# Attention rows of a four-layer GNN gathered in earlier stages; ScalarE copies the turned weights, Pool the node strips, key rows in bf16

## The reference

```
two_edge = concatenate(split(edge_attr, 2, axis=-1), axis=0)   # 50000 x 128
out_idx = concatenate([receivers, senders], axis=0)            # with 25000 edges of the record
logits = sum(two_edge * node_attr[out_idx], axis=1) / sqrt(128)
seg_max = segment_max(logits, out_idx)
ex = exp(logits - seg_max[out_idx])
denom = segment_sum(ex, out_idx)
agg = segment_sum(two_edge * ex / denom[out_idx], out_idx)
x = concatenate([agg, node_attr], axis=1) @ W + b
```

## Time and profile before

| | us |
|---|---|
| median of 3 runs | 6680.08 (6674.97 to 6690.29) |
| the profiled execution | 6675.12 |
| its span in the trace | 6673.5 |
| pair counts, 1453 to 1973 | 520 |
| source pass, each of three | 256 |
| GCN normalisation | 86 |
| attention side D, side S | 545, 544 |

### The profile page before, as it was taken

The page is one execution under the profiler, slowest core; times in us unless marked ns, Lnnn a source line. Parts: engine busy times, 40 slices in busy tenths (PEclk is TensorE's granted clock), DMA queues, the critical chain, the costliest instruction groups (busy, mean ns, idle before and its releaser), DMA issues. The chain is left out here.

```text
span 6673.5 us, 88566 instructions
## 1 busy us (share of the span) xinstructions
PE 3400.8 (51%) x20818; PEld 2597.0 (39%) x20821; DVE 3893.5 (58%) x13711; ACT 1143.2 (17%) x3927; POOL 3040.9 (46%) x3168
## 2 busy tenths in 40 slices
PE   1000200036644765466468889789567666632333
PEld 0000000024433554355345545455566656632333
DVE  9100910079985877577765473464677767774444
ACT  0000000015541111011100000000155545520000
POOL 2776277702323775477400000000077767724775
PEclk9999999978875555555578889789788878865555
DMA  6000000014443443344354464454043344311112
GB/s 281 3 3 20 6 3 3 3 46 132 133 117 80 106 105 61 85 102 102 53 114 89 86 130 84 82 114 89 12 108 105 98 98 104 105 30 40 50 49 45
DMA packets 802920, 512.99 MB, mean 77 GB/s; under 512 B 591282, under 2 KB 707036, under 8 KB 798684
## 3 DMA queue, kind: packets, MB, share of 16 engines
q1 hardware_dynamic: 702044, 351.52, 20.8%
q0 software_dynamic: 100608, 158.42, 11.2%
HBM read 384.62 MB, written 125.12 MB: 76 GB/s over the span
## 5 line engine op out<-in xcount | busy, mean ns | idle before, releaser
L738 POOL DMA_INDIRECT attD_g<-in_edge_attr,attD_ring x416 | 395.3, 950 | 1681.5 <-ACT attD_ring L752 1559.6
L738 POOL DMA_INDIRECT fild_g<-table,fild_ring x416 | 426.9, 1026 | 298.2 <-ACT fild_ring L752 173.0
L196 POOL DMA_INDIRECT recordsS<-sortS_rS,sortS_addrS x416 | 425.4, 1023 | 262.8 <-DVE sortS_addrS L237 136.4
L738 POOL DMA_INDIRECT gatBp_g<-table_head,gatBp_ring x416 | 415.2, 998 | 242.2 <-issue 124.6
L738 POOL DMA_INDIRECT gatAp_g<-table_heads,gatAp_ring x416 | 408.5, 982 | 251.4 <-ACT gatAp_ring L752 126.2
L196 POOL DMA_INDIRECT recordsD<-sortD_rD,sortD_addrD x392 | 401.2, 1023 | 221.8 <-issue 119.1
L738 POOL DMA_INDIRECT attS_g<-in_edge_attr,attS_ring x416 | 396.2, 952 | 149.7 <-issue 122.2
L802 PE MATMUL fild_ps<-fild_g,fild_oh 128*128 128x128 f32 x832 | 213.3, 438 | 394.3 <-DMA fild_g<-table,fild_ring 288.5
L698 PE MATMUL pairs_p_b<-pairs_blk,pairs_oh 128*128 128x256 f16 x1024 | 280.8, 304 | 184.5 <-DVE pairs_oh L685 165.1
L661 POOL DMA_DIRECT2D pairs<-pairs_blk x256 | 159.1, 622 | 431.4 <-ACT pairs_blk L713 422.0
L802 PEld LDWEIGHTS fild_ps<-fild_g,fild_oh 128*128 128x128 f32 x832 | 185.3, 328 | 422.2 <-DVE fild_oh L854 176.4
(11 more groups left out here) (655 smaller groups left out, 10291.6 us busy)
## 6 DMA issues: line engine op xcount, KB each, us to landing
gcnw_strip<-pairs SPq DMA_DIRECT2D x150, 800.0 KB, 5.9
pairs<-pairs_blk SPq DMA_DIRECT2D x768, 64.0 KB, 1.5
pairs<-sortD_blank SPq DMA_DIRECT2D x27, 1600.0 KB, 37.9
gatAp_rowb<-locD SPq DMA_DIRECT2D x104, 256.0 KB, 3.3
gatBp_rowb<-locD SPq DMA_DIRECT2D x104, 256.0 KB, 3.2
attD_rowb<-locD SPq DMA_DIRECT2D x104, 256.0 KB
attS_rowb<-locS SPq DMA_DIRECT2D x104, 256.0 KB, 3.4
pairs<-pairs_blk POOLq DMA_DIRECT2D x256, 64.0 KB, 1.9
```

The lines of the kernel that those rows point to most:

```text
L196: pool.indirect_dma_start(self.rec_dram, bass.IndirectOffsetOnAxis(ap=self.addr[:, c:c + 1], axis=0), self.r[:, c, :], None, bounds_check= ...
L738: pool.indirect_dma_start(rows(u, k), None, table, bass.IndirectOffsetOnAxis(ap=ring[:, u, k:k + 1], axis=0)).then_inc(gathered[u], 16)
```

## The change

All 832 attention gathers leave the attention passes. They are done in earlier stages, in groups of four as before (208 groups: 104 of side D, then 104 of side S), into a small ring `held_attr` in SBUF, and from there SP stores each group (256 KB) to a DRAM table `attrD` or `attrS`, in the order in which it is wanted. 56 groups go to the pair counts, 46 to each source pass, 14 to the GCN normalisation. The attention pass loads them back by plain DMAs of SP.

```
+FETCH = {"pairs": 56, "source": 46, "norm": 14}
+HOLD = {"pairs": 8, "source": 6, "norm": 6}
+    def gather(self, pool, k):
+        n = self.first + k
+        side, slot, turn = "DS"[n // NG], k % HOLD[self.kind], k // HOLD[self.kind]
+        if turn:
+            pool.wait_ge(self.put[slot], 16 * turn)
+        for q in range(G):
+            ...
+            pool.indirect_dma_start(self.held[:, slot, q, :], None, self.table,
+                                    bass.IndirectOffsetOnAxis(ap=rows, axis=0)).then_inc(self.landed[slot], 16)
+
+    def store(self, eng, k):
+        slot, turn = k % HOLD[self.kind], k // HOLD[self.kind]
+        eng.wait_ge(self.landed[slot], 16 * G * (turn + 1))
+        eng.dma_start(attr_group(self.C, self.first + k), self.held[:, slot]).then_inc(self.put[slot], 16)
+
+    def all_stored(self, eng):
+        for slot in range(HOLD[self.kind]):
+            eng.wait_ge(self.put[slot], 16 * len(range(slot, FETCH[self.kind], HOLD[self.kind])))
```

**Pair counts.** The loops of SP and Pool are written out. Pool, after its store of item g (and before it waits for item g + 1):

```
+                while done < (g + 1) * FETCH["pairs"] // NG_ITEMS:
+                    attr.gather(pool, done)
+                    done += 1
```

**Source passes and normalisation.** Pool runs `attr.gather(pool, k)` for k in 0 to 45 (0 to 13), and nothing else. SP stores between its strip loads:

```
             for i in range(LOADS, NT):
                 sp.wait_ge(summed, i - LOADS + 1)
                 sp.dma_start(held(i), by_source[i]).then_inc(strip_in[i % LOADS], 16)
+                while done < (i - LOADS) * FETCH["source"] // (NT - LOADS):
+                    attr.store(sp, done)
+                    done += 1
+            for k in range(done, FETCH["source"]):
+                attr.store(sp, k)
+            attr.all_stored(sp)
```

**Attention pass.** SP loads keys and rows into a slot; the keys are now bf16 (128 KB instead of 256 KB), as is `pen`:

```
+                    sp.wait_ge(pen_ready, nth(i - 1, u))
+                    sp.wait_ge(acc_done, nth(i - 1, u))
+                    load(i, u)
```

The node strips (`hts`) go from ACT to Pool, which waits for the products of two groups before. The copy of the turned weights (`wt`) goes from DVE to ACT, and the index copies (L752) are gone from here:

```
-            def take_weights(i, u):
-
-                dve.wait_ge(weights_turned, nth(i, u))
-                nc.vector.tensor_copy(wt[:, u % 2], p_w[:]).then_inc(wt_ready, 1)
...
+            def take_weights(i, u, before=U):
+                if before >= 2:
+                    act.wait_ge(acc_done, nth(*behind(i, u, -2)))
+                act.wait_ge(weights_turned, nth(i, u))
+                nc.scalar.copy(wt[:, u % 2], p_w[:]).then_inc(wt_ready, 1)
```

More of the change, by code:

```diff
@@ L648, in count_pairs @@
         block = ph.block()
[L650 to L664, removed]
+        attr = AttrFetch(nc, C, ph, a, "pairs", FIRST["pairs"])
         @block.sync
@@ L1066, in _, with attention_pass @@
             turns(pe, step)
-def attention_pass(nc, C, name, side, table, ht, acc, run, cont):
+def attention_pass(nc, C, name, side, ht, acc, run, cont):
     W = F + 1
@@ L1104, in _, with take_nodes, load @@
         def _(pool):
-            gather_groups(nc, pool, ring, indexed, table, lambda u, k: g[:, u, k, 0:F], gathered, acc_done)
+            def take_nodes(i, u, before=U, left=U):
+                nt = node_tiles(pool, C, side, i, u)
+                if before >= 2:
+                    pool.wait_ge(products, nth(*behind(i, u, -2)))
+                for k in range(G):
+                    last = nc.gpsimd.tensor_copy(hts[:, u % 2, k, :], ht[:, bass.ds(nt[k], 1), :].squeeze(1))
+                last.then_inc(hts_ready, 1)
+            turns(pool, take_nodes)
         @block.sync
         def _(sp):
-            load_key_rows(sp, C.loc[side], rowb, rows_loaded, pen_ready)
+            keys = C.loc[side]
+            def load(i, u):
+                loc = keys[tiles(i, u), :].rearrange("t p -> (t p)").partition_broadcast(P)
+                sp.dma_start(rowb[:, u, :], loc).then_inc(rows_loaded[u], 16)
+                rows = C.attr[side].rearrange("(n p g) f -> n p g f", p=P, g=G)[bass.ds(i * U + u, 1)].squeeze(0)
+                sp.dma_start(g[:, u, :, 0:F], rows).then_inc(gathered[u], 16)
+            for u in range(U):
+                load(0, u)
+            with sp.Fori(1, NG // U) as i:
+                for u in range(U):
+                    sp.wait_ge(pen_ready, nth(i - 1, u))
+                    sp.wait_ge(acc_done, nth(i - 1, u))
+                    load(i, u)
         @block.vector
@@ L1199, in take_rows, with step @@
                 nc.scalar.copy(gt[:, u % 2], p_g[u % 2][:]).then_inc(gt_ready, 1)
[L1201 to L1205, removed]
-            def step(i, u, before=U, left=U, index_next=True):
+            def take_weights(i, u, before=U):
+                if before >= 2:
+                    act.wait_ge(acc_done, nth(*behind(i, u, -2)))
+                act.wait_ge(weights_turned, nth(i, u))
+                nc.scalar.copy(wt[:, u % 2], p_w[:]).then_inc(wt_ready, 1)
+            def step(i, u, before=U, left=U):
                 if left >= 1:
-                    take_nodes(*behind(i, u, 1))
                     take_rows(*behind(i, u, 1))
@@ L1252, in multiply, with sums @@
                 last.then_inc(products, 1)
-            def sums(i, u):
+            def sums(i, u, before=U):
+                if before >= 2:
+                    pe.wait_ge(acc_set, nth(*behind(i, u, -2), G) + 1)
                 pe.wait_ge(wt_ready, nth(i, u))
@@ L1265, in step @@
                 if before >= 2:
-                    sums(*behind(i, u, -2))
+                    sums(*behind(i, u, -2), before=before - 2)
                 if before >= 1:
@@ L1731, in held, with _ @@
             return strip[:, (NT + i) % LOADS]
+        @block.gpsimd
+        def _(pool):
+            for k in range(FETCH["source"]):
+                attr.gather(pool, k)
         @block.sync
         def _(sp):
+            done = 0
             for i in range(LOADS, NT):
@@ L1911, in gcn_layers, with _ @@
             block = ph.block()
+            attr = AttrFetch(nc, C, ph, a, "norm", FIRST["norm"])
+            @block.gpsimd
+            def _(pool):
+                for k in range(FETCH["norm"]):
+                    attr.gather(pool, k)
+            @block.sync
+            def _(sp):
+                for k in range(FETCH["norm"]):
+                    attr.store(sp, k)
+                attr.all_stored(sp)
             @block.scalar
@@ L1984, in attention_layer @@
         for side in "DS":
[L1985 removed]
+            attention_pass(nc, C, name + side, side, ht, accs[side], run[side], cont[side])
         with Phase(nc, name + "a") as ph:
```

97 lines of the change are left out of this document (63 added, 34 removed).

## The result

The changed kernel takes 6447.7 us (median of 4 runs, 6446.6 to 6449.0), the kernel before 6679.2 us in the same comparison: ratio 0.9651, 95% interval 0.9634 to 0.9668. 231 us are gone, where 155 were forecast.

The account below looks back on a forecast made before the run. Pool's gathers were taken to bound both attention passes, DVE the pair counts. Attention -300, source passes +72, normalisation +28 and pair counts +45 gave -155 from 6675, or 6520, set at 6525 us for the median; range 6410 to 6790.

Parts of the forecast that it names:

- Attention, -150 each: Both attention passes: without Pool's gathers, 104 steps of 3.6 us plus 20 make 395 us instead of 545.
- The chain: Attention step: multiply, greatest, running maximum, then the next multiply; without the weight copy 3.3 us from group to group.
- a clock of 0.86: Attention passes: PE's average granted clock, making its 3.4 us of work 3.9; the step was taken as 3.6.
- The step of the weight copy: Attention step: the 0.68 us copy on DVE delays the first greatest; without it, that starts 0.1 us after the multiply.
- Pool's copies: Attention step: four copies on Pool at 0.293 us plus gaps, 1.2 to 2.4 us, under the 3.6 us step.
- The waits that were added: Attention passes: `acc_set` and `acc_done` look two groups back, cost nothing; up to 0.35 us per step if DVE fell behind.
- Source passes, +24 each: Three source passes: Pool does 6 groups, stops for the full ring, then does 40; 280 us instead of 256.
- Normalisation, +28: GCN normalisation: 16 DVE products each hold back a gather; 19 to 22 of 56 left over; ends +10 and +35.
- the tail, put at 4 us: End of the normalisation: a landing and a store, 4 us, behind 24 us of gathers left over.
- Pair counts, +45: Pair counts: DVE, the bound, delayed at most 0.23 us by each of 224 gathers, 52 us; ends 0 and +60.
- SP's loop: Pair counts: SP ended its stores 12.5 us after Pool's last; it gets 56 more issues but loses its loop.
- The starved gathers: Rival, pair counts: DVE's one-hots starve gathers, as one 21.0 us store suggests; +300 instead of +45, 6780 us; chance 0.27.

Follow-up runs that it names:

- the version without gathers: The kernel before, with only SP's and Pool's programs in the pair counts written out instead of looped, without a gather there: 6666.9 us, ratio 0.9988.

## Why the prediction was right, and where its terms were off

The forecast was 6525, in a range of 6410 to 6790, faster at 0.65; it came out 6448. The mechanism was right: the attention passes were bound by Pool's gathers, these fitted elsewhere, and what was lost elsewhere was a part of it. Part of the closeness is luck: the attention passes gave 49 us more than forecast and the pair counts took 41 less, while GAT and the normalisation took 19 more. By its steps:

- **Attention, -150 each; measured -174 and -175.** The chain was put at 3.3 us and steps of the changed kernel are 3.41 on average. The step that failed is the one after it, where 3.3 was raised to 3.6 for a clock of 0.86; that is 20 of the 24 us. That clock was one of the kernel before; it was 0.98 once PE no longer stood waiting for rows. It was read as a property of the work and is one of the waiting. That 3.41 lies near 3.3 does not show the chain at work: PE, busy 3.15 us per step, waits for its end in 13 steps of 104.
- **The step of the weight copy** was right in kind (it had to leave DVE) and wrong in reason. In the chain, as the prediction had it (the first greatest 0.35 us later), it would have cost 36 us per pass; in side D it cost 7. It was worth 97 us in side S, most likely for the fetches of code. The prediction had no such term, and as the change made the copy leave, this did not show in the result; with both copies at their old owners the kernel is at 6550.
- **Pool's copies** cost nothing, as said. The waits that were added were put at nothing too. They are met: `acc_set` holds PE's weight loads in 86 of 104 steps, 39.7 us in side D. Whether that lengthens the step was not tested.
- **Source passes, +24 each; measured +24, +24, +23.** Six groups, a stop of 36.2 us, then 40 groups: as worked out.
- **Normalisation, +28; measured +36**, just over the end of +35. 16 products held back 16 gathers, and 36 of the 56 were done when DVE ended, where 37 were forecast. The mis-sized term is the tail, put at 4 us: from the last gather's end at 4865.1 to the next stage at 4876 there are 11 us, for its landing (up to 9.9 us in this stage) and its store.
- **Pair counts, +45; measured +4.** The term was 0.2 us of DVE delay for each gather. DVE's busy time grew by 2.7 us in all. What the gathers do cost, 15 us, comes behind DVE: Pool's last store ends 7 us later than in the version without gathers, four gathers stand behind it for 5, and SP's stores run on to 1974.1, 6 us after them; from there to the next stage it is 3 us less. And 11 us came back: 8 from SP's loop, which the prediction named and did not count, and 3 as no store was held.
- **The starved gathers**, the rival on the slower side with 0.27, did not come: 977 ns in the median, 1061 at most. Its main row was one store out of 256. What it read in that row was right, as two more stores of the same kind show, each held until DVE stopped; what was wrong is to expect it of every gather. Beside one-hots of some 0.27 us nearly every gather and store gets in; beside products of 3.49 us none did.
- **GAT pass A, +17**, had no term in the sum. The keys in bf16 did it: 571 us with them, 555 and 552 without in two runs. In the changed kernel Pool's 416 gathers are busy 427.6 us there and 408.5 before. Two kernels with the same GAT code were at 566. The trace shows what they meet. 86 of the gathers take over 1.1 us, and each of them ends 0.7 to 0.9 us after one of DVE's two operations of 0.68 us with both inputs in SBUF: 42 after the product `gatAp_msg`, 44 after the comparison `gatAp_oh`. Before there were 52 such gathers, 11 of them after `gatAp_msg`. The shorter penalty moves DVE's work in time, and more gathers start beside that product; that this is the way from the one to the other is argued, not tested. One case:

```profile
2106.45 0.68 DVE L1030 TENSOR_TENSOR gatAp_msg<-gatAp_g,gatAp_msg 128x512 f32<-128x512 f32 x1
...
2106.69 1.26 POOL L796 DMA_INDIRECT gatAp_g<-table_heads,gatAp_ring  x1 [0.30 <-issue]
```

## What to carry to other kernels

A granted clock that is read from a stage bound by waiting is not the clock of that stage once the wait is gone; price the new step at both. When work is hung beside a stage that has room, look at who puts it away: in the source passes the buffer ring and the place of the stores in SP's order cost 68 us, and the gathers themselves next to nothing. When one odd row is set against 255 plain ones, ask how often it comes and not only whether it is real. And when a bound is taken away, look for stalls that it covered, in the rows that name no releaser.

## What the runs showed of the hardware

- A loop of DVE of 285 records stood for 5.1 to 7.6 us at each branch back in one place of the program (in three kernels) and not in another, with 60 packets on the "instruction" queue against 8. With 277 records it did not.
- A gather issued by Pool takes 0.94 us, 0.98 beside back-to-back one-hots of DVE, and 3.2 to 4.1 us when it meets one product of 3.49 us with both inputs in SBUF. Beside such operations of 0.68 us it takes up to 1.5 us. In both cases it ends some 0.8 us after the operation.
- A store issued by Pool was held for 19.1, 19.5 and 21.0 us beside back-to-back one-hots, until DVE stopped; 3 of 512 in the kernels where Pool ran a loop, none of 3072 where it did not.
- DVE's operation on 128x512 keys took 348 ns with bf16 in and out and 486 with float32. Of the 0.14 us a half was saved per attention step, and 17 us were lost in another pass.
